# DVE's first prefix softmaxes ahead of the experts' last sum, two weighted-sum banks exchanged, the first local squares one step sooner

## What is computed

```python
# layer 0: x += ga * linear_attention(h);  x += gb * experts(h)        16 experts, top 4, and a shared one
h = layernorm(x) * (1 + ca) + sa
x = x + ga * windowed_attention(h)       # 16 heads of 8, window 64, causal, and a prefix of 16 global keys:
    scores = concat([q @ k_prefix, q @ k_window]) * scale, masked to -1e9
    out = softmax(scores) @ concat([v_prefix, v_window]);  y = out @ w_out
h = layernorm(x) * (1 + cb) + sb
x = x + gb * local_transformer(h)        # depth 2: shift tokens, qkv, l2norm of q and k, rotary, local
                                         # attention (8 heads of 64), output projection, layernorm, gated ffn
```

## Time and profile before

| | |
|---|---|
| runs | 1357.42, 1361.44, 1361.47 us; median 1361.44 |
| profiled execution | 1357.41 us; its span 1355.6 us |
| busy | PE 93%, DVE 78%, ACT 64%, POOL 53% of the span |
| granted TensorE clock, mean | 0.976 |
| windowed attention, steps 0 to 127 | 283.13 us (first L1388) to 633.90 us (end of the last) |

### The profile page before, as it was taken

How to read it: one execution, slowest core, us unless ns; L and a number is a source line. 1 busy time by engine, 2 the same in 40 slices (tenths; PEclk the granted TensorE clock), 3 DMA queues, 4 the chain that set the end, 5 groups by cost and what they waited for, 6 DMA issues and landing times.

```text
span 1355.6 us, 39915 instructions
## 1 busy us (share of the span) xinstructions
PE 1262.8 (93%) x16229; PEld 987.2 (73%) x16229; DVE 1057.3 (78%) x2379; ACT 866.9 (64%) x2061; POOL 720.6 (53%) x591
## 2 busy tenths in 40 slices
PE   5869999989999999997999999989979999999897
PEld 5758888867677777775688888866557888887665
DVE  5958656647887887877899999976769999998586
ACT  5642232245666666664899999964459999998532
POOL 5512254532445534436887777853347777788110
PEclk9979999979999999998999999999999999999999
DMA  5032552202000000000000000010010000000011
GB/s 165 32 78 51 125 126 65 63 2 71 11 3 3 3 3 3 3 6 26 10 9 10 17 10 10 2 31 21 19 27 10 10 12 15 10 6 2 7 32 49
DMA packets 51675, 39.32 MB, mean 29 GB/s; under 512 B 30867, under 2 KB 41510, under 8 KB 51366
## 3 DMA queue, kind: packets, MB, share of 16 engines
q1 hardware_dynamic: 51056, 36.57, 10.6%
q10 hardware_dynamic: 438, 0.20, 0.1%
HBM read 28.10 MB, written 2.37 MB: 22 GB/s over the span
## 4 chain that ended last, share of the span: by engine, by line
PE 71%; DVE 16%; ACT 6%; POOL 3%; issue 3%; ACTq 0%; DVEq 0%; POOLq 0%
PE PS L2586 6%; PE PS L2506 5%; PE PS L1618 5%; PE PS L2479 4%; PE PS L2490 4%; PE PS L2526 4%; PE PS L2451 4%; PE PS L2417 4%; PE PS L1627 4%; PE PS L2595 3%; PE PS L2418 3%; PE PS L2419 3%; PE PS L590 3%; PE PS L1659 2%; DVE d_mx L1388 2%
## 5 line engine op out<-in xcount | busy, mean ns | idle before, releaser
L1964 POOL TENSOR_TENSOR turn<-qk,sinl 128x1024 f32<-128x1024 f32 x64 | 215.7, 3370 | 105.8 <-DVE qk L2102 105.8
L1957 POOL TENSOR_TENSOR rn<-ss,neghalf 128x16 f32<-128x16 f32 x64 | 209.3, 3270 | 33.1 <-DVE ss L2095 32.6
L2301 ACT ACTIVATE kx<-PS,e_mx 128x128 f32<-128x128 f32 x512 | 151.2, 371 | 18.7 <-DVE e_mx L2086 18.7
L1388 DVE TENSOR_REDUCE d_mx<-PS 128x4 f32<-128x576 f32 x128 | 96.6, 755 | 60.3 <-PE PS L1618 58.0
L788 ACT ACTIVATE m_work<-PS 128x512 f32<-128x512 f32 x72 | 43.0, 597 | 122.1 <-PE PS L570 122.1
L1516 ACT ACTIVATE pa<-PS 128x512 f32<-128x512 f32 x128 | 76.4, 597 | 62.9 <-PE PS L1627 62.7
L1059 DVE TENSOR_TENSOR m_work<-m_work,PS 128x512 f32<-128x512 f32 x72 | 49.3, 686 | 68.9 <-ACT m_work L788 67.9
L1618 PEld LDWEIGHTS PS<-kx,d_q 32*64 32x64 f32 x2048 | 67.0, 135 | 49.2 <-issue 33.7
L2086 DVE TENSOR_REDUCE e_mx<-PS 128x8 f32<-128x1024 f32 x64 | 78.2, 1222 | 29.6 <-PE PS L2479 29.6
L1618 PE MATMUL PS<-kx,d_q 32*64 32x256 f32 (+1 forms) x2048 | 99.1, 309 | 0.0
L1526 ACT ACTIVATE pm<-pm 128x512 f32<-128x512 f32 x128 | 80.6, 630 | 27.4 <-DVE pp L1393 26.7
(11 more groups left out here) (274 smaller groups left out, 3588.7 us busy)
## 6 DMA issues: line engine op xcount, KB each, us to landing
cb<-comb_rows SPq DMA_DIRECT2D x16, 512.0 KB, 8.8
Z<-comb_rows SPq DMA_DIRECT2D x16, 512.0 KB, 9.4
zs<-Z SPq DMA_DIRECT2D x64, 32.0 KB
out_x<-X SPq DMA_DIRECT2D x8, 256.0 KB, 2.4
zs<-Z SPq DMA_DIRECT2D x64, 31.8 KB
pa<-Z SPq DMA_DIRECT2D x16, 127.0 KB
X<-in_L_attn_x SPq DMA_DIRECT2D x3, 512.0 KB, 7.5
turn<-in_e_wqkv SPq DMA_DIRECT2D x2, 768.0 KB, 4.2
```

Of the source, the lines that this page charges most:

```text
L1388: chain(dve.tensor_reduce(mx[:, par, :, :], s, AX.X, ALU.max))
L1957: pool.tensor_tensor(rn[:, v % 2, :], ss[:, v % 2, :], c.neghalf[:, :], ALU.pow).then_inc(rn_ready.sem, 1)
L1964: pool.tensor_tensor(rot[:, :, :, :], x, bc(sinl[:, t, :, :], 2, H2), ALU.mult).then_inc(rot_ready.sem, 1)
L2301: last = act.activation(pm[:, v % 2, h, r, j, :], PS[:, SBANK + r, at * KEYS2:(at + 1) * KEYS2], ACT.Exp, bias=mx[:, v % 2, r, at:at + 1])
```

## The change

DVE does `softmax(0)`, `apply(2)`, `softmax(1)` in step 71 (before: `apply(2)`, `softmax(0)`), then, in the attention's loop, `softmax(2)`, and only then the experts' last sum `add(7)` and `stats(3)`. Before, the order was `add(7)`, `stats(3)`, `softmax(1)`, `softmax(2)`. So that PE need not wait for the sum, the weighted sums of even units go to bank 6 and those of odd units to bank 5: unit 0 now waits for the prefix work and unit 1 for the sum. The last unit (31) is thereby in bank 5, in whose last quarter `turn_z(0, 4)` writes; `turn_z(0, 4)` therefore waits for the last residual, and stands behind `project_v(0, 1)` and `hide(0, 0)`. ACT's `squares(0, 0)` goes from `ahead(123)` to `ahead(122)`. No instruction is added or taken away, and no DMA is moved.

```diff
@@ experts, DVE
-            add(NG8 - 1)
             settle, ahead, rest = last.vector(dve, steps)
-            main(settle, ahead)
+            main(settle, ahead, lambda: add(NG8 - 1))
@@ windowed attention: divide, resid, take_o, weigh, weigh_pre, turn_o, project
-            o = PS[:, UBANK + w % 2, 0:H1 * VW1].rearrange("p (h e) -> p h e", e=VW1)
+            o = PS[:, UBANK + (w + 1) % 2, 0:H1 * VW1].rearrange("p (h e) -> p h e", e=VW1)
...
@@ DVE
             if s == 71:
+                softmax(0)
                 apply(2)
-                softmax(0)
-
-        def main(settle, ahead):
-            dve.wait_ge(added.sem, added.at(2 * B))
+                softmax(1)
+
+        def main(settle, ahead, add_last):
             for u in range(U):
                 for s in range(STEPS):
-                    if u or s:
+                    if u or s > 1:
                         softmax(STEPS * u + s)
-                    if s == 0:
-                        if u and u + 2 < U:
+                    if u == 0 and s == 2:
+                        add_last()
+                        stats(3)
+                    if s == 0 and u:
+                        if u + 2 < U:
                             apply(u + 2)
@@ PE, weigh
             if k == 0:
+                pe.wait_ge(pre_done.sem, 2 * B)
+            if s == 0 and u == 1:
                 pe.wait_ge(added.sem, added.at(2 * B))
-            if s == 0 and u == 1:
-                pe.wait_ge(pre_done.sem, 2 * B)
@@ local transformer, ACT, ahead
-            if k in (AHEAD + 2, AHEAD + 3, AHEAD + 5):
+            if k in (AHEAD + 1, AHEAD + 3, AHEAD + 5):
                 squares(0, (k - AHEAD - 1) // 2)
@@ PE, turn_z
             elif v == B:
-                pe.wait_ge(done.resid.sem, done.resid.at(NT - 1))
+                pe.wait_ge(done.resid.sem, done.resid.at(NT))
@@ PE, rest
             project_v(0, 0)
-            turn_z(0, B)
             project_v(0, 1)
             hide(0, 0)
+            turn_z(0, B)
```

More of the change, by code:

```diff
@@ L1372, in resid @@
             dve.wait_ge(y_ready.sem, w + 1)
-            chain(dve.tensor_tensor(yg[:, w % 2, :], PS[:, UBANK + w % 2, Y0:Y0 + D], c.rowB[:, c.L1GA, b, :], ALU.mult))
+            chain(dve.tensor_tensor(yg[:, w % 2, :], PS[:, UBANK + (w + 1) % 2, Y0:Y0 + D], c.rowB[:, c.L1GA, b, :], ALU.mult))
             dve.tensor_tensor(xt(w), xt(w), yg[:, w % 2, :], ALU.add).then_inc(c.resid_done.sem, 1)
@@ L1511, in take_o @@
             act.wait_ge(oT_psum.sem, w + 1)
-            act.activation(oT[:, w % 2, :], PS[:, UBANK + w % 2, OT0:OT0 + P], ACT.Copy).then_inc(oT_ready.sem, 1)
+            act.activation(oT[:, w % 2, :], PS[:, UBANK + (w + 1) % 2, OT0:OT0 + P], ACT.Copy).then_inc(oT_ready.sem, 1)
         def take_p(k):
@@ L1647, in weigh @@
             g, e = s // 2, s % 2
-            ub = UBANK + u % 2
+            ub = UBANK + (u + 1) % 2
             pe.wait_ge(pT_ready.sem, k + 1)
             if k == 0:
+                pe.wait_ge(pre_done.sem, 2 * B)
+            if s == 0 and u == 1:
                 pe.wait_ge(added.sem, added.at(2 * B))
-            if s == 0 and u == 1:
-                pe.wait_ge(pre_done.sem, 2 * B)
             if s == 0 and u >= 2:
@@ L1669, in weigh_pre @@
                 pe.wait_ge(pre_done.sem, 2 * u + 2)
-            last = pe.matmul(PS[:, UBANK + u % 2, (g % 2) * n:(g % 2 + 1) * n], pb[:, g % 2, :],
+            last = pe.matmul(PS[:, UBANK + (u + 1) % 2, (g % 2) * n:(g % 2 + 1) * n], pb[:, g % 2, :],
                              vpre[:, b, g % 2, :, :].rearrange("p h e -> p (h e)"), start=False, stop=True,
@@ L1677, in turn_o @@
             pe.wait_ge(o_ready.sem, w + 1)
-            pe.transpose(PS[:, UBANK + w % 2, OT0:OT0 + P], on[:, w % 2, :, :].rearrange("p h e -> p (h e)"),
+            pe.transpose(PS[:, UBANK + (w + 1) % 2, OT0:OT0 + P], on[:, w % 2, :, :].rearrange("p h e -> p (h e)"),
                          ident[:, :]).then_inc(oT_psum.sem, 1)
@@ L1682, in project @@
             pe.wait_ge(oT_ready.sem, w + 1)
-            pe.matmul(PS[:, UBANK + w % 2, Y0:Y0 + D], oT[:, w % 2, :], wo[:, :], start=True, stop=True).then_inc(y_ready.sem, 1)
+            pe.matmul(PS[:, UBANK + (w + 1) % 2, Y0:Y0 + D], oT[:, w % 2, :], wo[:, :], start=True, stop=True).then_inc(y_ready.sem, 1)
         def first_t(b):
```

## The result

| | before | changed |
|---|---|---|
| median of the runs | 1361.47 us (8 runs) | 1346.13 us (8 runs) |
| lowest | 1355.14 us | 1342.98 us |
| profiled execution, its span | 1357.41, 1355.6 us | 1342.98, 1341.2 us |
| granted clock, mean | 0.976 | 0.987 |

The ratio is 0.9898, with a 95% interval of 0.9874 to 0.9923: faster by 1.0%. The forecast was 1346. The same kernel in another set (changed_again in the tables) gave 1345.21 (12 runs) against 1357.03 (32 runs of the kernel before), ratio 0.9953 (0.9932 to 0.9973). By the medians of all runs the differences are 15.3 and 11.8 us. The ratios are taken over the runs within 1.5% of the fastest of each kernel; what lies above is not in them.

The account below looks back on a forecast made before the run. PE was taken to set the pace, its half clock costing more than the gap before it. Terms 1.7 + 8.3 + 2.6 - 0.2 = 12.4 us, from 1357.41 to 1345.0, forecast as 1346; range 1343 to 1350, 8 in 10 1341 to 1355.

Parts of the forecast that it names:

- Term 1: Experts to windowed attention: softmaxes ahead of the sum cut PE's gap from 2.15 to 0.5 us, saving 1.7 us.
- Term 2: Windowed attention's start: with the shorter gap PE's clock does not fall to half for 20.5 us, saving 8.3 us.
- slower rival: Clock falls later, between 300 and 600 us, costing 5.5 us per unit at half; 1367 with four units; chance 0.04.
- Term 3: Start of the local transformer: earlier squares end DVE's 2.56 us wait, saving 2.6 us (bounds 2.2 and 2.65).
- The second rival: The second joint, at the local transformer's start, gives nothing: POOL's chain or the clock takes it back; 1349 us, chance 0.09.
- The coin: Second joint: if DVE's residual add starts before POOL's sine, up to 2.2 us more; counted as nothing, 1.3 in the range.
- Term 4: Ahead of the first local scores: turn_z(0, 4) in its later place costs 0.2 us (bounds nothing and 0.41).
- The sum's cover: First joint: the experts' last sum and stats(3) behind softmax(2) cost nothing; if uncovered, 1.2 us once.
- The rivals: Here first the one that the clock falls all the same after the first joint, leaving 4.1 us gain; 1354 us, chance 0.12.

Follow-up runs that it names:

- before_gap_filled: The kernel before, plus two 128x512 matmuls of no use in PE's 2.15 us gap ahead of step 1's transposes; median 1348.52 us against 1358.11, ratio 0.9952.
- before_look: The kernel before, unchanged, profiled once more; 1370.4 us, with a half-clock stretch of 58 us.
- second_joint_filled: The changed kernel plus three 128x512 matmuls of no use in PE's gaps ahead of the scores of steps 126 and 127; 1346.03 us, ratio 0.9939.
- turn_z_early: The changed kernel with turn_z(0, 4) back between project_v(0, 0) and project_v(0, 1), still waiting for the last residual; 1346.26 us, ratio 0.9951.
- sum_second: The changed kernel with the experts' last sum and stats(3) between softmax(1) and softmax(2) instead of behind softmax(2); 1345.62 us, ratio 0.9935.

## Why the prediction was right, by its steps

**Term 1 (1.7 us).** Right: 21.98 - 20.26 = 1.7 between the filled and the changed kernel. apply(2) took 0.34 us, not 1.17, since POOL's operation ended at 282.91, soon after apply(2) had started at 282.78, and softmax(1) did begin with its scores.

**Term 2 (8.3 us).** Right in size for the execution that was read: 8.6 by before_gap_filled. That the gap brings the fall is shown, by filling it and nothing else. PE took 5.2 us from the transposes of step 1 to the maxima of step 4 in that run (289.05 to 294.25), as the sum had it. One reading in it is off: the 15.7 us were not a unit at half throughout, since the clock was back at 311.1, before the unit's end at 312.94. A unit wholly at half took 16.9 us (before_look, 296.03 to 312.93). That moves only a bound of the term, 4.25 to 3.95, and the slower rival's price, 5.5 to 6.7 us for a unit. What the prediction missed is that this is a draw, one of several outcomes of the same program: behind the same gap the clock fell for 20.5 or 58 us, and behind one of 2.09 for 0 or 20.5. The profiled execution was of the middle group. Had it been one like before_look, the same sum would have given some 15 us more; with none, 4 in all. What parts 1357 from 1361, the two values that it left open, was not settled: no execution near 1361 was profiled. Short falls such as the one at 1266, which cost about 1.5 us, are too small for it alone. The longer half stretch at the experts' beginning, with the scores of step 0 near 286 in place of 282.4, has the right size, 3.6 us; that it is the cause is not shown.

**Term 3 (2.6 us).** 2.7 at step 127 in every pair of traces (24.36 and 21.67). At the first local maxima the pair before and changed has 1.4 left. PE's clock was at half from 613, and ACT waited for its projections of unit 3, 0.41 and 0.68 us. But how much is left differs by execution: with the squares late five traces take 38.82 to 40.84 us to these maxima (middle 40.64), with them early eight take 37.67 to 39.76 (middle 38.4), so that 2.2 is the better figure. The pair with the same half stretch ahead has 2.7. The second rival, that the clock takes the gain back, was right for a part: second_joint_filled puts it at 0.5 to 1.2 us. The coin fell against the add.

**Term 4 (-0.2 us).** Right: 0.2 by turn_z_early.

**The sum's cover.** Right, and with room: sum_second.

**The rivals.** The clock did not fall between 290 and 600 us in either of the changed kernel's profiles, and none of its 20 runs lies above 1352. The median was 1346.13, but part of that closeness is chance. Of the profiled difference 1.2 + 1.5 us are outside the change, and term 3 gave 1.2 less in this pair. The sum was taken from the fastest of three known runs, 1357.41; from their median, 1361.44, it gives 1349.0, and the only reason given for the first was that its execution had been read. And the gain between two medians, 15.3 us in one set and 11.8 in the other, depends on how many runs of the kernel before fell into which group, of which the sum knows nothing.

## What to carry to other kernels

Price an idle gap of PE with the clock behind it, in the windows, and not by its own length: here 1.7 us of gap went together with a tail of 8.6. Before a tail is believed, look at a second execution and at how the runs lie: groups of times with one program mean that the trace shows one draw. See also where two traces part ahead of the change, and compare stage by stage from there. To tell the clock's share from the schedule's, fill the gap with matmuls of no use and leave the order alone.

## What was not expected of the hardware

Once PE was at 1.2 GHz in this attention, it stayed there although it was busy in every microsecond, for 20.5 us in one execution and 58 in another, while behind a gap of 3.54 us it was back after 6.8. What ends such a stretch stays open: nearly the same work followed in all, only its place in time differed. At the first joint gaps of 0.48 and 1.10 us brought no fall, 2.09 and 2.15 one in four of five traces, and 3.54 in the one that was profiled. At the second joint the changed kernel's clock fell at 613.2, behind gaps of 1.29 us (until 610.83) and in one of 0.97 (until 613.59), so 1.1 us is no safe length in general. At the experts' beginning the half stretch was 3.4 us in one execution and 13.7 in another of the same instructions.
